# Row attention: bias, eviction and row minimum in one VectorE operation, and the next group norm's statistics taken inside the same loop

## The reference

```
x = x + attention(_gn(x));  x = x + scan_block(_gn(x))

# attention, N = 256, H = 4 heads of C = 32
scores = einsum('bijhd,bikhd->bijkh', q, k) * (1.0 / C ** 0.5)
scores = scores + bias[:, None, :, :, :]        # bias = zn @ Wb
a = softmax(scores, axis=-2)
o = sigmoid(zn @ Wg) * einsum('bijkh,bikhd->bijhd', a, v)
return o @ Wo

# _gn
m = mean(g, axis=(1, 2, 4));  s = var(g, axis=(1, 2, 4));  (g - m) / sqrt(s + eps)
```

## Time and profile before

| | |
|---|---|
| time, median of 3 runs | 24590.47 us (24589.01 to 24595.27) |
| profiled execution, its own time | 24590.69 us |
| span of that execution, first to last instruction | 24588.9 us |
| attention stage, from the first load to the end | about 581 to 2324 us |
| statistics of the second norm | about 2324 to 2437 us |
| convolution, scans, output | from 2437 us to the end |
| busy over the whole span | PE 95%, DVE 97%, ACT 94%, POOL 87% |

### The profile page before, as it was taken

How to read it: one execution, slowest core, us unless ns; L and a number is a source line. 1 busy time by engine, 2 the same in 40 slices (tenths; PEclk the granted TensorE clock), 3 DMA queues, 4 the chain that set the end, 5 groups by cost and what they waited for, 6 DMA issues and landing times. The chain is left out here.

```text
span 24588.9 us, 511985 instructions
## 1 busy us (share of the span) xinstructions
PE 23455.0 (95%) x191692; PEld 20535.8 (84%) x191692; DVE 23805.9 (97%) x23996; ACT 23008.6 (94%) x46999; POOL 21344.2 (87%) x9612
## 2 busy tenths in 40 slices
PE   4997989999999999999999999999999999999999
PEld 1775468888888888888888889999998999999887
DVE  6999889999999999999999999999999999999996
ACT  3997579999999999999999999999999999999986
POOL 5000049999999999999999999999999999999997
PEclk8998999999999999999999999999999999999999
DMA  5112555555555555555555555555555555555555
GB/s 184 58 59 92 178 183 173 172 174 172 173 174 173 170 186 187 187 185 187 186 187 188 182 184 187 187 186 187 185 187 181 187 186 187 185 187 187 186 185 190
DMA packets 2918646, 4287.93 MB, mean 174 GB/s; under 512 B 1199806, under 2 KB 2251106, under 8 KB 2636258
## 3 DMA queue, kind: packets, MB, share of 16 engines
q1 hardware_dynamic: 2916194, 4255.17, 52.0%
HBM read 3660.03 MB, written 594.54 MB: 173 GB/s over the span
## 5 line engine op out<-in xcount | busy, mean ns | idle before, releaser
L1352 DVE TENSOR_TENSOR_SCAN s_h<-s_da,s_h,s_db 128x512 f32<-128x512 f32 x16256 | 19261.5, 1314 | 0.5 <-PE s_db L1252 0.4
L1368 POOL TENSOR_TENSOR s_prod<-s_h,s_cb 128x2048 f32<-128x2048 f32 x4096 | 18772.5, 4583 | 7.6 <-issue 4.2
L1322 ACT ACTIVATE s_da<-s_delta,a_neg 128x512 f32<-128x512 f32 x16384 | 11290.9, 764 | 109.2 <-DVE s_h L1352 39.2
L1311 ACT ACTIVATE s_dxb<-s_dx,s_btok 128x256 f32<-128x256 f32 x20480 | 9422.1, 550 | 27.4 <-PEq L59 27.4
L1265 PE MATMUL s_py<-eye,s_prod 128*128 128x128 f32 x65536 | 8574.4, 274 | 104.1 <-POOL s_prod L1368 88.4
L1249 PE MATMUL s_db<-eye,s_dxb 128*128 128x128 f32 x49152 | 8214.2, 276 | 401.9 <-ACT s_dxb L1311 172.1
L1265 PEld LDWEIGHTS s_py<-eye,s_prod 128*128 128x128 f32 x65536 | 7363.9, 141 | 279.8 <-POOL s_prod L1368 185.9
L1249 PEld LDWEIGHTS s_db<-eye,s_dxb 128*128 128x128 f32 x49152 | 5816.3, 141 | 1702.9 <-issue 875.3
L1252 PE MATMUL s_db<-s_bdiag,s_dx 128*128 128x128 f32 x32768 | 6344.2, 275 | 0.0
L1252 PEld LDWEIGHTS s_db<-s_bdiag,s_dx 128*128 128x128 f32 x32768 | 4954.6, 191 | 0.0
L1381 POOL TENSOR_SCALAR s_dxb<-s_dx,s_btok 128x256 f32<-128x256 f32 x4096 | 2044.8, 499 | 75.8 <-POOLq L59 49.4
(11 more groups left out here) (135 smaller groups left out, 16695.2 us busy)
## 6 DMA issues: line engine op xcount, KB each, us to landing
s_cb<-c_rows SPq DMA_DIRECT2D x2048, 1024.0 KB, 4.8
s_bdiag<-b_diag SPq DMA_DIRECT2D x2048, 256.0 KB, 5.2
s_xt<-xc_tok SPq DMA_DIRECT2D x1024, 256.0 KB, 5.3
y<-s_yt SPq DMA_DIRECT2D x1024, 256.0 KB, 3.2
s_xc<-xc_own SPq DMA_DIRECT2D x384, 512.0 KB, 5.7
s_yb<-y SPq DMA_DIRECT2D x768, 256.0 KB, 4.4
xc_tok<-c_ot SPq DMA_DIRECT2D x32, 2048.0 KB, 8.7
xc_own<-s_xc SPq DMA_DIRECT2D x128, 512.0 KB, 5.5
```

The costliest lines, as they stand in the source:

```text
L1311: last = e.activation(dxb[:, i % NDXB, j, :], dx[:, g % 2, j, :], ACT.Copy, scale=btok[:, g % 2, j, n:n + 1])
L1322: last = e.activation(da[:, i % NDA, half, :], delta[:, g % 2, half, :], ACT.Exp, scale=wts[k]["a_neg"][:, half, n:n + 1])
L1352: last = e.tensor_tensor_scan(h[:, n, half, flow], da[:, i % NDA, half, flow], db[:, i % NDB, half, flow], first, ALU.mult, ALU.add)
L1368: e.tensor_tensor(prod[:, p % GROUPS_KEPT], h[:, states], cb[:, states, :].unsqueeze(2).to_broadcast([P, TOGETHER, HALVES, T]), ALU.mult). ...
```

## The change

1. `Wq` is multiplied once by -1/sqrt(32) and `Wb` by -1, both on DVE in the first block. The scores and the bias thus come out negated and scaled.
2. `biased` becomes two `tensor_tensor_reduce` per head, of 256 columns each: it adds bias and score, writes the sum, and writes the minimum of the row to `ntop`. The reduction at L521 and its signal `top` are gone. The exponentials take `scale=-1.0` and wait for `sev` of their head.
3. The copy of head 2 from `turn` moves from ACT to DVE, between `statistics` and `biased` of head 2.
4. `statistics` takes the second norm's `bn_stats` from `xt` in SBUF, in the attention loop: 4 instructions of 64 values in each turn, for the chunk of 8 rows that was finished in the turns before, and 32 behind the loop for the last chunk. SP waits for them (`stats`) before it loads a slot again. There are 32 parts for each group now, not 4.
5. `group_stats` is cut in two; for the second norm only `group_scales` (the joining and the chain behind it) is run. The first norm has one block more.

```diff
-                    e.scalar_tensor_tensor(
-                        out=sc[:, r % 3, h, :, :], in0=scores[:, h, :].rearrange("p (b k) -> p b k", b=JB), scalar=SCALE,
-                        in1=bias[:, :, h, :], op0=ALU.mult, op1=ALU.add).then_inc(S["sev"], 1)
+                    for jb in range(JB):
+                        last = e.tensor_tensor_reduce(
+                            out=sc[:, r % 3, h, jb, :], in0=scores[:, h, jb * SIDE:(jb + 1) * SIDE], in1=bias[:, jb, h, :],
+                            scale=1.0, scalar=FAR, op0=ALU.add, op1=ALU.min, accum_out=ntop[:, r % 3, h, jb:jb + 1])
+                    last.then_inc(S["sev"], 1)
+
+                def turned_copy(r, h):
+                    e.wait_ge(S["turned"], HEADS * r + h + 1)
+                    if r >= 2:
+                        e.wait_ge(S["pv"], r - 1)
+                    e.tensor_copy(pt[:, r % 2, h].rearrange("p b k -> p (b k)"), turn[:, h % 2, :]).then_inc(S["tev_dve"], 1)
+
+                def statistics(q, part):
+                    first = q % SLOTS * CHUNK
+                    if part == 0:
+                        e.wait_ge(S["yev"], (q + 1) * CHUNK)
+                    for g in range(part * GROUPS // CHUNK, (part + 1) * GROUPS // CHUNK):
+                        last = e.bn_stats(st[:, g, q, :], xt[:, first:first + CHUNK, :, g * PER_GROUP:(g + 1) * PER_GROUP]
+                                          .rearrange("p r b c -> p (r b) c"))
+                    if part == CHUNK - 1:
+                        last.then_inc(S["stats"], 1)
...
-                        e.wait_ge(S["turned"], HEADS * r + 1)
-                        if r >= 2:
-                            e.wait_ge(S["pv"], r - 1)
-                        e.tensor_copy(pt[:, r % 2, 0].rearrange("p b k -> p (b k)"), turn[:, 0, :]).then_inc(S["tev_dve"], 1)
+                        turned_copy(r, 0)
                     if 0 <= r + 2 < N:
                         biased(r + 2, 0)
                         biased(r + 2, 1)
...
+                        if q >= CHUNK:
+                            statistics(q // CHUNK - 1, q % CHUNK)
+                    if 0 <= r < N:
+                        turned_copy(r, 2)
                     if 0 <= r + 2 < N:
-                        q = r + 2
-                        biased(q, 2)
-                        biased(q, 3)
-                        e.wait_ge(S["sev"], HEADS * q + HEADS)
-                        if q >= 3:
-                            e.wait_ge(S["exp"], HEADS * (q - 3) + HEADS)
-                        e.tensor_reduce(ntop[:, q % 3], sc[:, q % 3], AX_X, ALU.max, negate=True).then_inc(S["top"], 1)
+                        biased(r + 2, 2)
+                        biased(r + 2, 3)
...
+                for part in range(CHUNK):
+                    statistics(N // CHUNK - 1, part)
...
# ACT
-                    e.wait_ge(S["top"], r + 1)
+                        e.wait_ge(S["sev"], HEADS * r + h + 1)
-                        turned_copy(r, 2)
                         turned_copy(r, 3)
# SP
+                        e.wait_ge(S["stats"], q + 1)
                         load(q + SLOTS)
# first block, DVE
+                e.tensor_scalar(wts["Wq"][:, :], wts["Wq"][:, :], -float(HEAD_DIM) ** -0.5, None, ALU.mult)
+                e.tensor_scalar(wts["Wb"][:, :], wts["Wb"][:, :], -1.0, None, ALU.mult)
# build
-        attention_phase(nc, sems, x, zn_t, bias_d, x1, wts, const)
-        group_stats(nc, sems, "g1", x1, 1e-5, const, scale_row, shift_row, (scale_col, shift_col))
+            attention_phase(nc, sems, x, zn_t, bias_d, x1, wts, const, st)
+            group_scales(nc, sems, "g1", st, 1e-5, const, scale_row, shift_row, (scale_col, shift_col))
```

More of the change, by code:

```diff
@@ L59, in end_block, with group_stats @@
     nc.all_engine_barrier()
-def group_stats(nc, sems, name, x, eps, const, scale_row, shift_row, columns=None):
+def group_stats(nc, sems, name, x, eps, const, scale_row, shift_row):
     CHUNK = BANK // PER_GROUP
@@ L70, in group_stats @@
         st = m.sb(f"{name}_st", [P, GROUPS, chunks, 6])
[L71 to L77, removed]
         src = x.rearrange("(p j k) c -> j p k c", p=P, k=CHUNK)
-        S = signals(sems, "load0 load1 stats aggr mean dev spread var std chain")
+        S = signals(sems, "load0 load1 stats")
         with nc.Block() as block:
@@ L95, in _, with group_scales @@
                     last.then_inc(S["stats"], 1)
-                e.wait_ge(S["stats"], chunks)
+        end_block(nc, sems)
+        group_scales(nc, sems, name, st, eps, const, scale_row, shift_row)
+def group_scales(nc, sems, name, st, eps, const, scale_row, shift_row, columns=None):
+    with ExitStack() as stack:
+        m = Memory(nc, stack)
+        mv = m.sb(f"{name}_mv", [P, GROUPS, 2])
+        avg = m.sb(f"{name}_avg", [P, GROUPS, 2])
+        dev = m.sb(f"{name}_dev", [P, GROUPS])
+        var = m.sb(f"{name}_var", [P, GROUPS])
+        std = m.sb(f"{name}_std", [P, GROUPS])
+        pick = m.sb(f"{name}_pick", [P, 2, GROUPS])
+        total = m.ps(f"{name}_total", [P, 2, BANK])
+        S = signals(sems, "aggr mean dev spread var std chain")
+        with nc.Block() as block:
+            @block.vector
+            def _(e):
                 for g in range(GROUPS):
@@ L278, in norm_phase, with attention_phase @@
         end_block(nc, sems)
-def attention_phase(nc, sems, x, zn_t, bias_d, x1, wts, const):
+def attention_phase(nc, sems, x, zn_t, bias_d, x1, wts, const, st):
     N = SIDE
@@ L285, in attention_phase @@
     SLOTS = 4
-    SCALE = float(HEAD_DIM) ** -0.5
+    FAR = 3.0e38
     NV = 4
@@ L324, in attention_phase @@
         S = signals(sems, "loadz0 loadz1 loadz2 loadz3 loadx0 loadx1 loadx2 loadx3 store0 store1 store2 store3 "
-                          "qk qkev vg gate vev score sev top exp turned tev_dve tev_act pv rden spread across factor gated ymm yev")
+                          "qk qkev vg gate vev score sev exp turned tev_dve tev_act pv rden spread across factor gated ymm yev stats")
         def turned_out(e, r, h):
-            if h == 0:
-                e.wait_ge(S["tev_dve"], r + 1)
+            if h % 2 == 0:
+                e.wait_ge(S["tev_dve"], HEADS // 2 * r + h // 2 + 1)
             else:
-                e.wait_ge(S["tev_act"], (HEADS - 1) * r + h)
+                e.wait_ge(S["tev_act"], HEADS // 2 * r + h // 2 + 1)
         with nc.Block() as block:
@@ L453, in exponent @@
                     for h in heads:
+                        e.wait_ge(S["sev"], HEADS * r + h + 1)
                         for jb in range(JB):
                             last = e.activation(sc[:, r % 3, h, jb, :], sc[:, r % 3, h, jb, :], ACT.Exp,
-                                                bias=ntop[:, r % 3, h, jb:jb + 1], accum_out=den[:, r % 2, jb, h:h + 1])
+                                                bias=ntop[:, r % 3, h, jb:jb + 1], scale=-1.0, accum_out=den[:, r % 2, jb, h:h + 1])
                         last.then_inc(S["exp"], 1)
@@ L1680, in build @@
         norm_phase(nc, sems, x, zn_t, bias_d, wts, const, scale_row, shift_row)
-        attention_phase(nc, sems, x, zn_t, bias_d, x1, wts, const)
-        group_stats(nc, sems, "g1", x1, 1e-5, const, scale_row, shift_row, (scale_col, shift_col))
+        with ExitStack() as inner:
+            st = Memory(nc, inner).sb("g1_st", [P, GROUPS, SIDE // 8, 6])
+            attention_phase(nc, sems, x, zn_t, bias_d, x1, wts, const, st)
+            group_scales(nc, sems, "g1", st, 1e-5, const, scale_row, shift_row, (scale_col, shift_col))
         conv_phase(nc, sems, x1, xc_tok, xc_own, wts, const, scale_col, shift_col)
```

## The result

The changed kernel takes 24666.35 us, median of 8 runs (24659.12 to 24670.16), against 24592.87 us for the kernel before in 8 runs (24588.96 to 24598.53): a ratio of 1.003, 95% interval 1.002 to 1.0039. It is slower by 73 us. The profiled execution took 24659.12 us, 68.4 more than that of before, and it is split by stage. A stage begins here with its own first load, so attention begins at 575.3 us before, with the loading of the bias.

A forecast was written before the change was run, and what follows sets the result against it. Three nearly full engines bound attention at 6.71 us a turn; the change would close a chain of waits between PE and DVE. 24590.7 + 213 (attention) - 87.5 (second norm) + 1.2 (small) = 24717 us, range 24605 to 24850.

The forecast's parts named there:

- T: Time of one fused tensor_tensor_reduce of 256 columns on DVE in the attention loop, forecast at 0.44 us.
- The ring's form: Attention turn: PE's scores, DVE's evictions, sum, statistics and head 2's copy, then mix_values and next transposes; 7.56 us, +213 us.
- rival A: Row minimum in the fused eviction nearly free, 0.33 to 0.37 us an operation; 24604 to 24645 us, chance 0.13.
- The hand-over: From the end of DVE's copy of head 2 to PE's mix_values, 0.15 us, taken from ACT's copy.
- The copy: Head 2's copy on DVE in the attention loop, ahead of mix_values, forecast at 0.64 us a turn.
- The joining: Second norm: bn_aggr over 32 parts, 0.62 us each, 19.9 us in place of 4.0; stage -87.5 us.
- Small terms: Two more operations in the first block and one more barrier in the first norm, together +1.2 us.
- ACT's relief: Attention loop: ACT loses one copy, 0.5 us a turn, worth nothing because PE's order is longer.
- DVE's load: DVE's work in an attention turn, hardly relieved: from 6.52 to 6.47 us.
- Rival D: Attention loop faster because the chain of waits does not bind; 24504 us, or 24376 if PE has room; chance 0.07.

The follow-up runs named there:

- the last experiment: Against the kernel with head 2's copy on ACT and statistics over chunk pairs: that copy on DVE again, ahead of head 1's eviction; 24477.16 us, ratio 0.9954 to before.
- the first experiment: Changed kernel with the copy of head 2 put back on ACT, in its old place; 24509.92 us, ratio 0.9967 to the kernel before.

## Why the prediction was right, and where its sum was off

The direction, the mechanism and the order of the waits came out as written: the turn rose from 6.71 to 7.32 where 7.56 was forecast, the time by 73 us (68 in the profiled execution) where 126 was. The sign and the range held. Luck has a part in this. The time falls just inside the 24655 to 24780 that the forecast gave to T from 0.38 to 0.50, while T was 0.345, below it; the terms below say how. Point by point:

- **The ring's form.** Right in each link: 2.18 and 1.98 on PE, 0.34 for the sum, 0.51 for the statistics, and `mix_values` waiting for DVE's copy of head 2. Three runs show it that no load theory explains: the same instructions reordered (127 us less), extra work inside the ring (129 us more) and outside it (8 us more).
- **T, the price of the fused operation.** This is the term that failed: 0.345 us, not 0.44. The read of the accumulator is a separate instruction, as ACT's rows suggested and as the Trainium skill says (VectorE: DVE Perf Modes, "Two Vector instructions with no wait between them"); the trace agrees, with a read of 0.08 us. But it starts with the next operation and adds 0.01 us, not 0.11. The case that happened is rival A, to which I gave 0.13. The four in the ring make 0.38 us a turn, 97 us in all. The nearest row was chosen for the extra instruction's own cost in a full queue; what no row could tell is that it overlaps the next one. Only the upper half of my bounds rested on ACT, whose read does hold up the next activation (0.50 against 0.27).
- **The hand-over.** 0.26, not 0.15: +0.11 a turn, 28 us. I took ACT's hand-over for DVE's. The engine made no difference; the position of the wait did, as the run with the reordered waits shows.
- **The copy.** 0.68 behind another DVE instruction, not the 0.64 of the earlier trace rows: 10 us.
- **The joining.** `bn_aggr` of 32 parts took 0.885 us each, not 0.62, so the second norm's stage gave back 79 us, not 87.5. My slope came from 1 and 4 parts (0.018 a part); between 4, 16 and 32 parts it is 0.027.
- **Small terms.** -5 us ahead of the attention stage where +1.2 was forecast; 3.6 of it lie in `norm_phase`, which the change doesn't touch. The attention stage begins anywhere from 569.9 to 577.0 us in the runs here, at 572.4 with the copy of head 2 alone, which changes nothing ahead of it; so this is a spread between executions, and its cause is open.

The errors together: 24717 - 97 + 28 + 10 + 8 - 6 = 24660, against the profiled execution's 24659.12. So the forecast was 58 us off and not 97, by luck: three smaller errors went the other way. Rival A, whose T was the true one, would have given some 24620, too low by these same three.

**The ring through ACT.** The prediction called ACT's relief worth nothing, because PE's order was the longer one. In the changed kernel that held: PE waits there for DVE, and ACT idles 0.97 us a turn (over 1.4 was forecast). But PE's order was not what held 6.71 before. Once the ring through DVE is open, one copy less on ACT brings 0.08 us a turn, 19 us, as the last experiment shows.

**DVE's load.** Forecast as hardly relieved, 6.47 us. With T = 0.345 it is 5.7, and DVE idles 1.4 us a turn. (The T up to which DVE would stay below the ring comes out at 0.71 from the prediction's own terms, not 0.69; nothing rests on it.)

**Rival D (faster, 24504 if the ring did not bind)** is what the first experiment made: 24510. The lower figure of 24376, by which PE would have room because its weight loads are busy for only 76% of the stage, did not come in any run. With both rings open the turn stopped at 6.63, with the matmuls busy for 671 of 671 us and the loads of weights for 517. As far as 6.63 is PE's own length, the matmuls' busy time was the better guide to the room left in this loop, and the Trainium skill's rule (Perfetto Trace Analysis, "Identifying the Most-Contended Engine"), which sets it aside for MFU and the loads of weights, was not. The same skill's advice to restructure `tensor_reduce` (VectorE: DVE Perf Modes, "Rules for kernel authors") took away a reduction of 2.2 us a turn and, alone, changed nothing: 1.5 us of 24591, one execution each.

## What to carry to other kernels

When engines run hand-ordered loops, a piece of work moved to an engine with room must be placed by what stands in front of it in that engine's order: if that needs something the waiting engine makes in the same turn, a ring is closed, and every instruction inside it costs its full time even while both engines idle. Sum each ring from the starts in one turn of the trace, before and after the move; the longest sum is the turn. The cure can be order alone: here the copy ahead of the statistics took back 127 us without a change to any instruction. The copy ahead of one head's eviction too, with the statistics over pairs (worth 14 us), turned a loss of 73 us into a gain of 110.

## What the runs showed of the hardware that I had not expected

- The read of DVE's accumulator (0.08 us long) starts together with the next DVE operation: 0.345 us from one fused operation of 256 columns to the next, against 0.33 for a plain one. ACT's read of its accumulator adds 0.23.
- `bn_aggr` costs more for each further part when there are many: 0.018 us between 1 and 4 parts, 0.027 from 4 to 32. In all 0.073 us for 1, 0.126 for 4, 0.451 for 16 (14.44 / 32), 0.885 for 32 (28.31 / 32).
- A wait that is already met still costs PE 0.11 us when it stands behind the one that arrives last (0.26 us from the copy's end to `mix_values`, 0.15 with the two waits swapped).
